# Scan units placed in steps by a table: three in each Silu step, none beside the second block's projections

## The reference

```python
x = x + _L0_conv_ref(_gn(x), ...)   # first block
x = x + _L1_conv_ref(_gn(x), ...)   # second block
```

```python
h = jnp.exp(d_t[..., None] * A) * h + (d_t * x_t)[..., None] * b_t[:, None, :]
y_t = jnp.einsum('bdn,bn->bd', h, c_t)
```

## Time and profile before

| | |
|---|---|
| three runs | 3494.55, 3541.34, 3560.41 us (median 3541.34) |
| profiled execution | 3522.22 us, span 3520.5 us |
| PE | 3085.5 us busy (88%), 19488 instructions |
| PEld | 1739.0 us (49%) |
| DVE | 2682.1 us (76%), 3980 instructions |
| ACT | 1843.2 us (52%), 4315 instructions |
| POOL | 1774.9 us (50%), 1347 instructions |
| granted TensorE clock, mean | 0.921 |
| DMA | 290.86 MB, queue q1 27.4% of 16 engines |

### The profile page before, as it was taken

One profiled execution on the slowest core, in us unless ns is written; L12 is line 12 of the kernel. 1 busy time (PEld: TensorE's weight loads), 2 busy tenths in 40 slices (PEclk: granted clock), 3 DMA queues, 4 the chain that ended last, 5 costly groups with the idle time before them and its releaser, 6 DMA issues. The chain is left out here.

```text
span 3520.5 us, 59688 instructions
## 1 busy us (share of the span) xinstructions
PE 3085.5 (88%) x19488; PEld 1739.0 (49%) x19488; DVE 2682.1 (76%) x3980; ACT 1843.2 (52%) x4315; POOL 1774.9 (50%) x1347
## 2 busy tenths in 40 slices
PE   4988889998898998889898898988889998898965
PEld 2655446364453735447364453735446364453710
DVE  1448878788787867868789787878868788787887
ACT  1536464653646546464564646546464563746542
POOL 2216545464554535545364554646545464555655
PEclk9999999998999989989899989989999998999976
DMA  3032141423214142141423314142141423215131
GB/s 63 11 108 75 46 129 50 116 70 97 85 46 144 40 136 65 58 116 39 134 70 96 85 46 127 58 129 76 59 117 46 121 70 108 73 45 147 37 103 66
DMA packets 103726, 290.86 MB, mean 83 GB/s; under 512 B 24941, under 2 KB 26588, under 8 KB 103388
## 3 DMA queue, kind: packets, MB, share of 16 engines
q1 hardware_dynamic: 103388, 286.71, 27.4%
HBM read 181.84 MB, written 39.85 MB: 63 GB/s over the span
## 5 line engine op out<-in xcount | busy, mean ns | idle before, releaser
L768 POOL TENSOR_TENSOR hc<-hst,bcrep 128x512 f32<-128x512 f32 x768 | 1204.4, 1568 | 1165.7 <-DVE hst L1249 1118.7
L854 ACT ACTIVATE ssd<-bank,ncs 128x128 f32<-128x128 f32 x1536 | 439.4, 385 | 230.1 <-PE bank L1298 229.3
L1298 PE MATMUL bank<-hc,sel 128*32 128x512 f32 x1536 | 447.7, 668 | 99.8 <-POOL hc L768 99.1
L1236 DVE TENSOR_TENSOR wr<-durep,bcrep 128x512 f32<-128x512 f32 x768 | 530.3, 691 | 3.1 <-DMA bcrep<-bc_rows 3.1
L1249 DVE TENSOR_TENSOR_SCAN hst<-dec,wr 128x512 f32<-128x512 f32 x256 | 389.7, 1522 | 93.6 <-ACT carry L999 60.3
L1298 PE MATMUL bank<-ssd 128*128 128x32 f32 (+1 forms) x3296 | 459.8, 293 | 0.0
L1298 PEld LDWEIGHTS bank<-ssd 128*128 128x128 f32 x3296 | 409.1, 197 | 17.6 <-issue 12.8
L958 ACT ACTIVATE bank<-durep,aneg 128x512 f32<-128x512 f32 x368 | 254.0, 690 | 300.4 <-DVE hst L1249 284.6
L1298 PE MATMUL bank<-ssd,wcv 64*32 64x512 f32 x5376 | 349.4, 599 | 0.0
L1298 PE MATMUL bank<-xna,wt0a 128*128 128x128 f32 (+3 forms) x1088 | 299.3, 377 | 36.4 <-DVE xnb L1064 35.4
L1249 DVE TENSOR_TENSOR_SCAN hst<-bank,carry,wr 128x512 f32<-128x512 f32 x240 | 306.1, 1275 | 11.9 <-ACT bank L958 2.5
(11 more groups left out here) (186 smaller groups left out, 4937.8 us busy)
## 6 DMA issues: line engine op xcount, KB each, us to landing
durep<-scratch SPq DMA_DIRECT2D x192, 512.0 KB, 3.9
bcrep<-bc_rows SPq DMA_DIRECT2D x128, 512.0 KB, 5.1
ssd<-stage SPq DMA_DIRECT2D x384, 140.4 KB, 2.9
ssd<-bcst SPq DMA_DIRECT2D x128, 74.4 KB, 2.7
xa<-in_x_dram SPq DMA_DIRECT2D x16, 512.0 KB, 4.2
scratch<-u SPq DMA_DIRECT2D x32, 256.0 KB, 2.5
scratch<-delta SPq DMA_DIRECT2D x32, 256.0 KB, 2.8
out_dram<-x1a SPq DMA_DIRECT2D x16, 512.0 KB, 4.6
```

The lines of the kernel that those rows point to most:

```text
L768: nc.gpsimd.tensor_tensor(hc[:, i % CRING, :], hst[:, i % HRING, :], bcrep[:, g, 1, :], ALU.mult).then_inc(hc_ready.sem, 1)
L854: ins = nc.scalar.activation(att[:, c % 2, h, :], bank[ROW_BANKS[r]][:, k * Q:(k + 1) * Q], ACT.Exp, bias=ncs[:, c, h:h + 1])
L1236: nc.vector.tensor_tensor(wr[:, i % WRING, :], durep[:, j % SLOTS_DU, 1, :], bcrep[:, g, 0, :], ALU.mult).then_inc(w_made.sem, 1)
L1298: return nc.tensor.matmul(out, lhsT, rhs, start=start, stop=stop, skip_group_check=True)
```

## The change

- The number of steps stays at 48, but a table, UNITS_IN_STEP, says how many units stand in each: one in most, three in steps 4, 6, 8 and 11, none in steps 40 to 47. Step s from 12 to 39 has unit s+8 where it had unit s. Every engine takes the units of a step one after the other, with the same operations, ahead of the step's first-block work (ScalarE's carries and copies: behind it).
- END_AT goes from (37, 10) to (30, 7). TensorE's wait ahead of half 1 is now for the scan of ten units; its wait ahead of half 0 for the scan of 36 units is gone, and finish of half 0 stands behind first_block in a step. ScalarE's copy_wide waits for the output's matmuls that read y1a.
- Decays in banks 0 and 1: units 0 to 9 and 44 to 47; all others in the SBUF ring. The wait for row_exp at unit 31 goes; the waits at units 38 and 39 go to 44 and 45.
- ScalarE's Abs, Exp and Ln of dt stand ahead of the Silu copies of step 4; TensorE's cumulative sums stand at step 5; the statistics of the next image's load (EARLY_AT) at step 41.

```diff
-SLOTS = UNITS
+STEPS = 48
+UNITS_IN_STEP = [1, 1, 1, 1, 3, 1, 3, 1, 3, 1, 1, 3] + 28 * [1] + 8 * [0]
+UNITS_AT = [range(sum(UNITS_IN_STEP[:s]), sum(UNITS_IN_STEP[:s + 1])) for s in range(STEPS)]
...
-EARLY_AT = 42
-
-END_AT = (37, 10)
+EARLY_AT = 41
+
+END_AT = (30, 7)
...
+FRONT_UNITS, LAST_UNITS = 10, 44
 def decay_bank(i):
-    if i < 8 or i >= 38:
+    if i < FRONT_UNITS or i >= LAST_UNITS:
         return i % 2
-    return 6 + i % 2 if 31 <= i < 36 else None
+    return None
...
@@ scalar, first_block @@
-                for u, at in enumerate(CONV_AT):
-                    if s == at + 1:
-                        copy_conv(n, u)
                 if s == 4:
...
                     nc.scalar.activation(dtl[:, :, :], dte[:, :, :], ACT.Ln, bias=1.0).then_inc(dtl_ready.sem, 1)
+                for u, at in enumerate(CONV_AT):
+                    if s == at + 1:
+                        copy_conv(n, u)
...
-                if first and i == 31:
-                    act.wait_ge(row_exp.sem, row_exp.at(n + 1, NRB * NCH))
-                if first and i == 38:
+                if first and i == LAST_UNITS:
                     act.wait_ge(gated.sem, gated.at(n + 1, NCH))
...
-            def copy_wide(n, hf):
+            def copy_wide(n, hf, prev):
+                if hf or prev:
+                    act.wait_ge(o1_ps.sem, o1_ps.at(n, 2 * hf))
...
@@ scalar, run @@
-                        decay(b, s, end, first)
+                        for i in UNITS_AT[s]:
+                            decay(b, i, end, first)
...
-                        if 2 <= s < HU + 2:
-                            act.wait_ge(scanned.sem, scanned.at(b, s - 1))
-                            nc.scalar.copy(carry[:, s - 2:s - 1], hst[:, (s - 2) % HRING, HALF - 1:HALF]).then_inc(carried.sem, 1)
+                        for i in UNITS_AT[s]:
+                            if 2 <= i < HU + 2:
+                                act.wait_ge(scanned.sem, scanned.at(b, i - 1))
+                                nc.scalar.copy(carry[:, i - 2:i - 1], hst[:, (i - 2) % HRING, HALF - 1:HALF]).then_inc(carried.sem, 1)
...
@@ vector, run @@
-                    elif scan:
-                        scan_unit(b, s - 1, end)
+                    for i in UNITS_AT[s]:
+                        if i == 0:
+                            if end:
+                                scan_unit(b - 1, UNITS - 1, False)
+                        elif scan:
+                            scan_unit(b, i - 1, end)
+                        if scan:
+                            inputs(b, i, end)
...
@@ tensor @@
-                if s == 6:
+                if s == 5:
                     pe.wait_ge(da_ready.sem, da_ready.at(n, 1))
...
+            def sums(b, i, scan, end):
+                if i in (0, BATCH):
+                    if end:
+                        sum_states(b - 1, BATCHES - 2 + i // BATCH, False)
+                elif scan and i > 2 and (i - 2) % BATCH == 0:
+                    sum_states(b, (i - 2) // BATCH - 1, end)
+                for hf in range(2):
+                    if scan and i == hf * HU + WIDE + 3:
+                        start_rest(b, hf)
...
+                    for i in UNITS_AT[s]:
+                        sums(b, i, scan, end)
                     if end:
                         if scan and s == END_AT[1]:
-                            pe.wait_ge(scanned.sem, scanned.at(b, 8))
+                            pe.wait_ge(scanned.sem, scanned.at(b, FRONT_UNITS))
...
-                        if s == END_AT[0]:
-                            pe.wait_ge(scanned.sem, scanned.at(b, 36))
-                        finish(b, s, 0, par)
                     if first:
                         first_block(b + 1, s, end if scan else None)
+                    if scan:
+                        finish(b, s, 0, par)
```

More of the change, by code:

```diff
@@ L56 @@
 UNITS = 2 * HU
-SLOTS = UNITS
+STEPS = 48
+UNITS_IN_STEP = [1, 1, 1, 1, 3, 1, 3, 1, 3, 1, 1, 3] + 28 * [1] + 8 * [0]
+assert len(UNITS_IN_STEP) == STEPS and sum(UNITS_IN_STEP) == UNITS
+UNITS_AT = [range(sum(UNITS_IN_STEP[:s]), sum(UNITS_IN_STEP[:s + 1])) for s in range(STEPS)]
 FILLS = 9
@@ L599, in traffic @@
             def traffic(b, par, scan, end, first, load_next):
-                for s in range(SLOTS):
+                for s in range(STEPS):
                     if end and s == OUT_AT:
@@ L616, in traffic @@
                             keep_rows(1)
-                        reads(b, s, par, end)
+                        for i in UNITS_AT[s]:
+                            reads(b, i, par, end)
                     if load_next and s == PRE_AT + 2:
@@ L771, in run @@
             def run(b, par, scan, end, first, more):
-                for s in range(SLOTS if scan or first else 2):
-                    if s < 2:
-                        if end:
-                            states_by_c(b - 1, UNITS - 2 + s, False)
-                    elif scan:
-                        states_by_c(b, s - 2, end)
+                for s in range(STEPS if scan or first else 2):
+                    for i in UNITS_AT[s]:
+                        if i < 2:
+                            if end:
+                                states_by_c(b - 1, UNITS - 2 + i, False)
+                        elif scan:
+                            states_by_c(b, i - 2, end)
                     if scan:
@@ L987, in run @@
                 mid_step = Steps(act, act_mid_steps, b)
-                for s in range(SLOTS if scan or first else END_AT[1] + END_STEPS):
+                for s in range(STEPS if scan or first else END_AT[1] + END_STEPS):
                     if scan:
-                        decay(b, s, end, first)
+                        for i in UNITS_AT[s]:
+                            decay(b, i, end, first)
                     if scan:
@@ L1260, in run @@
                 mid_step = Steps(dve, dve_mid_steps, b)
-                for s in range(SLOTS if scan or first else END_AT[1] + END_STEPS):
+                for s in range(STEPS if scan or first else END_AT[1] + END_STEPS):
                     if first:
                         first_block_soon(b + 1, s, step, 1 - par, scan, end)
-                    if s == 0:
-                        if end:
-                            scan_unit(b - 1, UNITS - 1, False)
-                    elif scan:
-                        scan_unit(b, s - 1, end)
+                    for i in UNITS_AT[s]:
+                        if i == 0:
+                            if end:
+                                scan_unit(b - 1, UNITS - 1, False)
+                        elif scan:
+                            scan_unit(b, i - 1, end)
+                        if scan:
+                            inputs(b, i, end)
                     if scan:
-                        inputs(b, s, end)
                         for piece in (MID, 2):
@@ L1577, in finish @@
                     mm(o, wo1b[r, c], y1b[r, :], False, True).then_inc(o1_ps.sem, 1)
-            def run(b, par, scan, end, first, more):
-                for s in range(SLOTS if scan or first else END_AT[1] + END_STEPS):
-                    if s in (0, BATCH):
-                        if end:
-                            sum_states(b - 1, BATCHES - 2 + s // BATCH, False)
-                    elif scan and s > 2 and (s - 2) % BATCH == 0:
-                        sum_states(b, (s - 2) // BATCH - 1, end)
-                    for hf in range(2):
-                        if scan and s == hf * HU + WIDE + 3:
-                            start_rest(b, hf)
+            def sums(b, i, scan, end):
+                if i in (0, BATCH):
+                    if end:
+                        sum_states(b - 1, BATCHES - 2 + i // BATCH, False)
+                elif scan and i > 2 and (i - 2) % BATCH == 0:
+                    sum_states(b, (i - 2) // BATCH - 1, end)
+                for hf in range(2):
+                    if scan and i == hf * HU + WIDE + 3:
+                        start_rest(b, hf)
+            def run(b, par, scan, end, first, more):
+                for s in range(STEPS if scan or first else END_AT[1] + END_STEPS):
+                    for i in UNITS_AT[s]:
+                        sums(b, i, scan, end)
                     if end:
                         if scan and s == END_AT[1]:
-                            pe.wait_ge(scanned.sem, scanned.at(b, 8))
+                            pe.wait_ge(scanned.sem, scanned.at(b, FRONT_UNITS))
                         if not scan and s == END_AT[1]:
```

11 lines of the change are left out of this document (5 added, 6 removed).

## The result

The changed kernel takes 3873.24 us (median of 4 runs, 3866.82 to 3875.80), the kernel before 3535.35 in the same comparison (4 runs, 3494.55 to 3560.41): ratio 1.0964, 95% interval 1.092 to 1.1009. The profiled execution has a span of 3865.1 us at a mean granted clock of 0.865 (0.921 before). The prediction had the sign and the order of the events, and its range (3590 to 3880) holds the time, but only just: the likeliest number, 3775, is 98 us too low and its own range (to 3840) does not hold it. The rival with the clock (3850) is nearest; that it comes so near is in part luck, as the account term by term shows.

The account below looks back on a forecast made before the run. It took TensorE to set the time, busy 189 of 208 us a pass. Terms 20.6 - 7.0 + 2.9 - 1.1 - 1.5 + 2.5 gave +16.4 a pass, +246 over fifteen passes, 3775 us; range 3590 to 3880.

Parts of the forecast that it names:

- The rival with the clock: After waits of 3 us or more TensorE first runs at 1.2 GHz: +21.9 us a pass, 3850; chance 0.18.
- The relay: Conv stage: scans wait for carries behind Silu copies, which stand behind decays waiting for earlier scans; TensorE waits 18.3 us.
- work that moves there: Conv stage: four sums of two units (4.0 us) and the narrow sum's opening come to TensorE: +5.0 a pass.
- (8): TensorE rows behind four idle gaps run slower at a lower clock: 0 to +8 us a pass, taken +2.5.
- (1): Projection stage without units takes 23.0 us: -7.0 a pass, ends -5.1 and -10.4.
- (2): Output of half 0 moves from steps 37 to 40 into 30 to 33, delaying the first block's last projection: +2.9 a pass.
- (3): The narrow sum's opening leaves step 19: -1.1 us a pass.
- (4): The SSD stage starts with VectorE ahead rather than behind: 0 to -3 us a pass, taken -1.5.
- (5): Nine units' decays leave PSUM for SBUF, nearly all beside SSD work: 0 us a pass, 2.7 if that cover went.
- (7): The dropped wait for scan 35 and the swap of first_block and finish: 0 to -0.5 us a pass, taken 0.
- half of it bites: Rival: only the conv-stage waits of steps 6 and 7 stay: +3.0 us a pass, 3567, no change; chance 0.11.
- The waits do not bite: Rival: the conv stage grows by 2.3 us for the work only: -7.8 a pass, 3405, faster; chance 0.06.

Follow-up runs that it names:

- carry kernel: The changed kernel with ScalarE's carry copies issued ahead of its first-block work and so of the Silu copies: 3582.35 us, ratio 1.0126.
- before-carry kernel: The kernel before the change with ScalarE's carry copy ahead of the first block's work: 3539.36 us, ratio 1.0004.
- filler run: The changed kernel with extra unused TensorE matmuls put into its four long waits of the conv stage: 3791.05 us, ratio 1.0709.
- two units in eight steps: The changed kernel with two units in each of steps 4 to 11 in place of three in 4, 6, 8 and 11: 3688.29 us, ratio 1.042.
- units in the SSD stage: The changed kernel with the eight units in eight steps of the SSD stage, one a step in the conv stage, 6 decays in banks: 3792.02 us.
- four-unit kernel: The changed kernel with half of the units moved (four), 8 decays in banks 0 and 1, output of half 0 at step 34: 3589.05 us.
- its sister with the carry ahead: The four-unit kernel with the carry copies ahead of the Silu copies: 3559.69 us, ratio 1.0046.
- eight decays besides: The changed kernel with the carry copies ahead of the Silu copies and 8 decays in banks 0 and 1 instead of 10: 3627.48 us.
- all three remedies: The changed kernel with two units in each of steps 4 to 11, 8 decays in banks and the carry copies ahead of the Silu copies: 3645.80 us.
- the even table besides: The changed kernel with two units in each of steps 4 to 11 and the carry copies ahead, 10 decays in banks: 3666.33 us, ratio 1.034.

## Why the prediction was right, and where its sizes were off

**The mechanism was right.** The relay, the two waits in it with their releasers, and the 58 us to the SSD stage were said before the result; the trace has the waits in order and, in this pass, 66.4 us. Step by step against the prediction's clock (its times less 95.72, so that the first convolutions coincide): scan 5 was to start at 1650.1 (1650.14), the second detour to end at 1665.2 (1666.00), scan 9 to end at 1667.4 (1668.06), u2 to start at 1668.5 (1670.34), the SSD stage at 1698.3 (1706.64). Up to scan 9 the working is off by 0.8 at most; behind it the distance grows to 8.3, in a stretch where TensorE's rows are slow. The carry kernel shows the cause (19.7 of 22.5 us), the before-carry kernel that it needs several units in a step.

**Term by term, a pass:**

| term | predicted | measured |
|---|---|---|
| waits in the conv stage, less those of before | +15.6 | +16.1 |
| work that moves there | +5.0 | +3.6 (filler run: 59.1 - 4.5 - 15.7 = 38.9 busy, 35.3 before) |
| clock in the gaps (8), conv stage alone | +2.5 | +7.9 |
| projection stage (1) | -7.0 | -9.6 |
| output moved (2) | +2.9 | +2.2 alone |
| SSD stage and tail by the rest (3), (4), (5), (7) | -2.6 | +2.3 (4.4 less 2.1) |
| sum | +16.4 | +22.5 |

**The term that was mis-sized most is (8).** I had the four gaps with 0 to +8 and took 2.5; in the pass shown the two convolutions alone cost 1.5 each, and the sums, x1a and y1a rows 0.9 to 1.0 each. The filler run puts the cost at 7.9, which is the clock rival's 8, and the SSD stage pays 5.0 more, as shown below. That rival's total (+21.9 for 22.5) is so near because its other terms missed in both directions: the SSD stage by +4.9, the projections by -2.6, the work by -1.4. I had weighed against the row that stayed fast behind 2.71; all of the gaps here were longer, 3.34 to 5.18, and each of them was followed by slow rows. So the nearest rows were those of the earlier trace rows, and the term should have come from them. The Trainium skill (TensorE: Matmul & The Clock Gate, What's actually happening) has the idle array at half clock by default; the rows behind these four gaps agree.

**(1) was too cautious**: TensorE waits 0.30 for gq and not 1.2 (I take it that the softplus no longer stands behind scans; no run shows that apart), and the end of the range that I had given for "nothing waits" (-10.4) was nearly met. But little of the 9.6 could ever be won. TensorE's own work that left the stage is 6.0 of it: 3.0 of the output's projection, 2.0 of sums and 1.0 of the narrow sum's opening, all to be done in another stage. Only the waits (3.4 to 0.3 us a pass) and rows at the low clock were there to be saved.

**(3), (4), (5) and (7) together** were off by 4.9. The SSD stage does not start with VectorE ahead: TensorE waits 3.33 for its state and runs slow behind that:

```profile
1718.50 1.65 PE L1310 MATMUL bank<-state,cs_ 128*128 128x384 f32 x2 [3.33 <-DVE state L1089]
...
1721.22 5.17 PE L1310 MATMUL bank<-ssd 128*128 128x32 f32 x24
```

In the kernel before the wait at this place was 2.48, and the rows behind it ran at the full clock:

```profile
1783.85 0.91 PE L1298 MATMUL bank<-state,cs_ 128*128 128x384 f32 x2 [2.48 <-DVE state L1079]
...
1785.25 2.76 PE L1298 MATMUL bank<-ssd 128*128 128x32 f32 x24
```

In the changed kernel VectorE is still at scans that the last carries held up (7.51 before the one at 1702.16). In the kernel with the carry ahead the same wait is 0.24 in all but the last pass, in the one with two units in eight steps 0.8 in the mean, and in both the 24 matmuls take 2.76; their stage and tail take 118.2 and 119.1, and the terms of the prediction give 119.6 + 2.9 - 2.6 = 119.9. The filler run, whose scans come late too, has the 3.33 in each pass and 126.6.

How the 5.8 us to the carry kernel (124.0 - 118.2) are made up shows in the means of 13 passes: TensorE is idle only 0.9 longer in the stage, as a later wait for the state gets shorter, but busy 5.0 longer (112.5 for 107.5) with the same matmuls, at a granted clock of 0.91 for 0.95. So the terms hold where the scans are in time. The start of the SSD stage, (4), had the wrong sign, and nearly all of its price is again the low clock: 7.9 in the conv stage and 5.0 here, 12.9 a pass where the sum had 2.5.

**The rival "half of it bites"** falls, all four waits were there. "The waits do not bite" is nearest to the carry kernel, which still has 10.0 us of waits: the order was most of the loss, but not all of it, as its conv stage takes 52.6 against 38.0 + 3.6.

## What to carry to other kernels

A small copy that closes a loop between two in-order queues should stand ahead of any long group in its queue when several turns of the loop fall in one step. With one turn in a step its place made no difference here, so look for it when a table packs turns together. Idle time of one engine (VectorE's 16 us) is room only for work that doesn't need a busy engine in each turn. Before you empty a stage, take out of its length the work of the busiest engine that has to go elsewhere: of 30 us here, 3.4 were waits. Remedies found one by one don't add up in such a loop: each moves the wait to another place, and four units in the stage cost 3 us where eight cost 28.

## What the runs showed of the hardware

- **Scans from SBUF beside GpSimd.** In the changed kernel 213 of the 544 scans that read the decay from SBUF took over 1.7 us (2.06 in the mean), the others 1.2 to 1.5; in the kernel before 94 of 400, with the units in the SSD stage 316 of 608. Scans from a bank stay at 1.22 to 1.28. VectorE's time in scans grows from 1043.5 to 1136.4 and 1214.4 us, which (5) had at nothing in the sum. GpSimd's product by C in the same stretch of the changed kernel:

```profile
1668.14 1.62 POOL L775 TENSOR_TENSOR hc<-hst,bcrep 128x512 f32<-128x512 f32 x1 [5.29 <-DVE hst L1259]
1671.01 1.55 POOL L775 TENSOR_TENSOR hc<-hst,bcrep 128x512 f32<-128x512 f32 x1 [1.24 <-DVE hst L1259]
```

The scan at 1668.82 began 0.94 before the end of the first product (1669.76) and took 0.81 longer than 1.22; the one at 1672.77 began behind the end of the second (1672.56) and took 1.21. The Trainium skill (SBUF — State Buffer, SBUF: two separate sides) says that a VectorE operation with two inputs in SBUF and a GpSimd operation that reads SBUF exclude each other, the second one waiting until the first has ended. The trace agrees within 0.15 us: in all 213 of the long scans a product was running when the scan began, and each took longer than 1.22 by what was left of that product, less 0.13 to 0.15. It shows the other way round too: GpSimd's product takes 1.3 us where no such operation of VectorE is running at its start (76 of them), and about 1.55 where 0.4 us of one are left, as at 1671.01. When scans stand close together, each meets the product of the scan before it; that is how units packed into a full stretch get dearer.

- **The clock.** Each gap of 3.3 to 5.2 us in the stage shown was followed by rows at the 1.2 GHz level (1.92 for 1.05, 6.89 for 5.38), the gap of 1.17 by none (0.46, as in the earlier trace rows). Behind 3.06 us of idle time the four-unit kernel kept its clock (a convolution of 5.38), and its sister with the carry ahead did not, behind the same 3.06:

```profile
1546.94 1.13 PE L1310 MATMUL bank<-x1a,ident 128*128 128x512 f32 x2 [3.06 <-DVE hst L1259]
...
1548.11 5.38 PE L1310 MATMUL bank<-ssd,wcv 64*32 64x512 f32 x96
```

```profile
1545.06 1.13 PE L1312 MATMUL bank<-x1a,ident 128*128 128x512 f32 x2 [3.06 <-DVE hst L1261]
...
1546.23 7.08 PE L1312 MATMUL bank<-ssd,wcv 64*32 64x512 f32 x96
```

The same wait went both ways. It did so in the SSD stage too. There the kernels with eight units moved and the carry ahead have a wait of 3.0 to 3.1 us for the state in each of the 13 passes; the rows right behind it ran at the low level in 5 of 13 passes with the carry ahead, in 9 with eight decays besides, in 12 with all three remedies and in 13 with the even table besides. In the carry kernel the stage and tail take about 116 us in eight passes and 122.4 in four. What decides it no run here shows, and the 3 us in the rival's condition are no limit: the slow convolution of the earlier trace rows stood behind 2.51.
